# The own-row term of the node update as one 128-column matmul per pair, first of its group

## The chip, the cores and the metric

The kernel runs on one core of one Trainium2 chip. The metric is the device time of one execution in microseconds (us), lower is better. The engines are PE (matrix products; PEld is its loading of weights), DVE (vector), ACT (scalar), POOL (indirect DMAs here) and SP (DMA queue).

## The reference

A graph network of four layers over 6250 nodes of 64 features and 206250 edges sorted by destination. In each layer:

```
msg  = concat(h[src], h[dst]) @ WM + bM
mean, mx, mn, std, var, s = aggregates of msg over the edges of each destination node
agg  = concat(mean, mx, mn, std, var, s)
hu   = concat(h, agg, agg * amp, agg * att) @ WU + bU        # amp, att: one number per node
hbn  = batchnorm(hu / sqrt(n));  hm = leaky_relu(hbn @ Wmix + bmix)
h    = relu(batchnorm(hm + h)) + h
```

The first 64 rows of WU multiply the node's own row h; this product is what the change moves. The other 1152 rows multiply the aggregates, plain and scaled by amp and att.

## The kernel before, in words

The 6250 nodes are 50 tiles of 125. A tile j of the first half (j = 0 to 24) and its counterpart of the second half stand together as pair j: the transposed features hT hold the one in partitions 0 to 63 and the other in 64 to 127, and the weight blocks for the own row (W from column W_U0, 128 columns) and for the destination term (from W_BB) are block diagonal, so that 64 columns belong to each half a = 0, 1.

A layer has a dense stage (one-hot products on PE, running maxima on DVE, gathers by POOL) and then the node stage, the subject here: 25 pairs, unrolled in program order on each engine, followed by two batch norms. Layer 0 is written out by itself; layers 1 to 3 are one body in a hardware loop over l. There every semaphore wait compares with a register worked out from l, and the helper `wait` (L389 to L393) puts one more instruction, an increment of `passed`, behind each such wait. In layer 0 the values are constants and nothing is put behind.

For each pair PE runs, in this order (L1898 to L1906):
- `columns(j + 2)`: four transposes of the dense maxima and sums (L1854), then the destination product (L1858), which signals `t_ps`;
- `update(j, 0)`: waits for `hut_ev` (pair j - 2's result has been read out of the bank that is about to be written) and for `at_ev` (the transposed aggregates have been copied to SBUF), then three matmuls of 192 columns (L1882) and one of 64 columns (L1884);
- `features(j + 1)`: six transposes of the next pair's aggregates (L1870);
- `update(j, 1)`: the same four matmuls for the other half; the last one signals `u_ps`;
- `back(j - 1)`: waits for `hu_done`, then one transpose (L1893), which signals `ht_ps`.

A fp32 matmul appears as two passes in the trace (L1884: 4 layers x 25 pairs x 2 halves = 200 matmuls, 400 rows); a transpose as one.

DVE runs `gather_up(j + 3, j)` (L1548 to L1593): L1573 to L1592 gather the aggregates of pair j + 3 once `t_ps` is there, and between them L1538, L1543 and L1546 combine the update of pair j (`u_ps`) into hu and signal `hu_done`. ACT runs per pair the squares and roots (`moments`, L739 to L743), the copy of the transposed aggregates to SBUF (L751, `at_ev`), the read-out of the transposed result (L761, with its accumulator read; `hut_ev`) and a square of it (L770). In ACT's order L751 of pair j stands ahead of L761 of pair j - 2.

UPS are two PSUM banks used in turn: columns 0 to 191 of a bank belong to half 0 and 192 to 383 to half 1; of each 192, the first 64 take the own row. HPS, the transposed result, lies in the same bank behind them.

Of the kernel before, what the change touches and what calls it, by code (L numbers as in the profile page):

```python
# [12 lines left out]
P = 128  # L13
N = 6250
E = 206250
D = 64
# [7 lines left out]
NP = 125  # L24
# [116 lines left out]
W_BB, W_U0, W_MIX, W_BM, W_U, W_COL = 0, 128, 256, 384, 448, 1024  # L141
# [26 lines left out]
def build(nc, x, src, dst, WM, bM, WU, bU, gamma_t, beta_t, Wmix, bmix, gamma_o, beta_o, out):  # L168
# [14 lines left out]
    with ExitStack() as ctx:  # L183
        def sb(name, shape, dt=F32):
            return ctx.enter_context(nc.sbuf_tensor(name, shape, dt))
# [10 lines left out]
        hT = sb("hT", [P, FC])  # L196
# [3 lines left out]
        W = sb("W", [P, W_ALL])  # L200
# [29 lines left out]
        TPS, UPS, BPS = [bank[0], bank[1]], [bank[4], bank[5]], bank[6]  # L230
# [42 lines left out]
        aggT = [[v[:, k * 3 * NP:(k + 1) * 3 * NP] for k in range(2)] for v in (flat_rows, spare)]  # L273
# [115 lines left out]
        def wait(eng, s, value):  # L389

            wait_at(eng, s, value)
            if not isinstance(value, int):
                eng.sem_inc(S["passed"])  # L393

        def wait_at(eng, s, value):

            eng.wait_ge(S[s] if isinstance(s, str) else s, value)
# [1276 lines left out]
        def _(pe):  # L1674
# [18 lines left out]
            for m in range(BATCHES):  # L1693
# [3 lines left out]
                for j in range(j0, j0 + n):  # L1697
                    ins = nc.tensor.matmul(bank[m % 2][:, (j - j0) * NP:(j - j0 + 1) * NP], codev[0:NP, j, :], identb[0:NP, 0:NP],
                                           start=True, stop=True)
# [3 lines left out]
            for k in range(TILES):  # L1703
                pe.wait_ge(S["e_ready"], k + 1)
                row0 = 64 * (k // VROWS) + k % VROWS
                for m, r in enumerate(STEPS):
                    ins = nc.tensor.matmul(bank[m][:, 0:r.stop - r.start], SELW[:, SEL - row0:SEL - row0 + P], EB[k % EBLK][:, r],
                                           start=k == 0, stop=k == TILES - 1)
# [6 lines left out]
            for k in range(SCAN_CHUNKS):  # L1715
                nc.tensor.matmul(bank[k][:, 0:SCAN], ones_bf[:, :], onehot[:, k * SCAN:(k + 1) * SCAN],
                                 start=True, stop=True).then_inc(S["ps1"], 1)
            for k in range(SCAN_CHUNKS):
                pe.wait_ge(S["ps1_used"], k + 1)
                nc.tensor.matmul(bank[k][:, 0:SCAN], below_bf[:, :], onehot[:, k * SCAN:(k + 1) * SCAN],  # L1720
                                 start=True, stop=True).then_inc(S["ps2"], 1)
# [9 lines left out]
            def layer(l, stored):  # L1731
# [142 lines left out]
                def update(j, a):  # L1874

                    i = l * HALF + j
                    if a == 0 and j >= 2:
                        wait(pe, "hut_ev", i - 1)
                    wait(pe, "at_ev", 2 * i + a + 1)
                    u = UPS[j % 2][0:NP, a * 192:(a + 1) * 192]  # L1880
                    for c in range(3):
                        nc.tensor.matmul(u, aggT[j % 2][a][:, c * NP:(c + 1) * NP], W[:, W_U + c * 192:W_U + (c + 1) * 192],  # L1882
                                         start=a == 0 and c == 0, stop=False, skip_group_check=True)
                    ins = nc.tensor.matmul(u[:, 0:D], hT[:, j * NP:(j + 1) * NP], W[:, W_U0 + a * D:W_U0 + (a + 1) * D],  # L1884
                                           start=False, stop=a == 1, skip_group_check=True)
                    if a:
                        ins.then_inc(S["u_ps"], 1)

# [9 lines left out]
                for j in range(HALF):  # L1898
                    if j + 2 < HALF:
                        columns(j + 2)  # L1900
                    update(j, 0)
                    if j + 1 < HALF:
                        features(j + 1)
                    update(j, 1)
                    if j >= 1:
                        back(j - 1)  # L1906
# [46 lines left out]
```

## Time and profile before

| | |
|---|---|
| median of 3 runs | 3956.39 us (3953.85 to 3956.59) |
| profiled execution, span from first to last instruction | 3968.1 us (the page gives no other time for it) |
| PE busy | 3314.0 us, 84% |
| DVE busy | 3137.6 us, 79% |
| POOL busy | 2223.3 us, 56% |
| ACT busy | 1168.6 us, 29% |
| mean granted PE clock | 0.958 of full |

Busy shares are means over stages that have different limits. The node stages lie at about 1234 to 1349, 2077 to 2201, 2939 to 3063 and 3796 to 3920 us. In rows of a timeline, "x6" means six instructions in a row merged, with the start of the first; their durations overlap, so that the pace is read from one start to the next. In brackets stands how long the engine was idle before and who released it.

### The profile page before, as it was taken

The numbers are of one execution on the slowest core, as the hardware profiler recorded it, in microseconds if no ns is written. First come the engines' busy times: TensorE is split into PE (matmuls) and PEld (weight loads), VectorE is DVE, ScalarE is ACT, GpSimd is POOL, SyncE is SP. The second block draws the span as 40 slices with busy tenths as digits, with TensorE's granted clock in tenths as the row PEclk, the third lists the DMA queues.
The fourth block names the chain that finished last, engine by engine and source line by source line (L and its number), as shares of the span: only waits on it lengthen the run. The fifth ranks groups of instructions, "written<-read, shape, count | busy, mean of one in ns | idle before, by whom it ended". The sixth has DMA issues, their size and how long they took to land.

```text
span 3968.1 us, 88783 instructions
## 1 busy us (share of the span) xinstructions
PE 3314.0 (84%) x29640; PEld 2061.9 (52%) x29640; DVE 3137.6 (79%) x6027; ACT 1168.6 (29%) x3428; POOL 2223.3 (56%) x2221
## 2 busy tenths in 40 slices
PE   0055699898887799999998699999988799999986
PEld 0022344444446657555558456555557466655575
DVE  6598588788776778888877678888876788888876
ACT  4302122222223612222225322222225332222243
POOL 6402577666654037777753147777750177777640
PEclk9997899999998899999999899999999899999997
DMA  7003799889896056556672256566670366566750
GB/s 209 16 0 81 217 257 258 239 247 254 248 258 210 14 163 178 175 173 191 201 232 77 79 157 178 170 175 191 198 240 16 118 174 180 170 189 189 219 163 34
DMA packets 300094, 668.65 MB, mean 169 GB/s; under 512 B 81751, under 2 KB 180237, under 8 KB 296995
## 3 DMA queue, kind: packets, MB, share of 16 engines
q1 hardware_dynamic: 188676, 419.32, 35.4%
q0 software_dynamic: 78400, 192.26, 18.5%
q10 hardware_dynamic: 32732, 54.15, 3.9%
q14 instruction: 216, 1.77, 0.1%
q8 instruction: 70, 1.15, 0.1%
HBM read 517.78 MB, written 151.72 MB: 169 GB/s over the span
## 4 chain that ended last, share of the span: by engine, by line
PE 21%; issue 20%; DMA 18%; DVE 12%; POOL 12%; ACT 2%; SPq 1%; DVEq 1%; ACTq 0%; POOLq 0%
POOL rows L881 11%; DMA rows<-table,lists 10%; PE bank L1815 8%; DMA RE<-vd 6%; PE bank L1789 4%; PE bank L1882 4%; DVE accL L1438 2%; DVE scr L1361 2%; PE bank L1798 2%; DVE scr L1372 1%; DVE accL L1434 1%; PE bank L1870 1%; DMA RE<-ohd 1%; DMA left<-accL 1%; SPq L476 1%
## 5 line engine op out<-in xcount | busy, mean ns | idle before, releaser
L881 POOL DMA_INDIRECT rows<-table,lists x1828 | 1833.0, 1003 | 836.6 <-issue 518.1
L1815 PE MATMUL bank<-RE,split 125*64 125x482 bf16 x15600 | 1846.5, 370 | 18.9 <-ACT scr L605 18.9
L1815 PEld LDWEIGHTS bank<-RE,split 125*64 125x64 bf16 x15600 | 948.9, 111 | 691.0 <-issue 34.2
L632 ACT ACTIVATE split<-rows,masks 128x128 f32<-128x128 f32 x1828 | 600.1, 391 | 1693.5 <-DMA rows<-table,lists 1311.9
L1789 PE MATMUL bank<-RE,split 126*64 126x482 bf16 x7800 | 924.2, 372 | 79.8 <-DVE scr L1372 60.4
L1361 DVE TENSOR_TENSOR scr<-scr,bank 128x964 f32<-128x964 f32 x624 | 692.1, 1109 | 78.8 <-PE bank L1789 74.0
L1372 DVE TENSOR_TENSOR scr<-scr,bank 128x964 f32<-128x964 f32 x624 | 692.0, 1109 | 45.0 <-PE bank L1798 40.0
L1789 PEld LDWEIGHTS bank<-RE,split 126*64 126x64 bf16 x7800 | 471.6, 111 | 430.5 <-DVE scr L1372 67.1
L1798 PE MATMUL bank<-RE,flip_w 126*64 126x482 bf16 x2600 | 391.4, 373 | 112.8 <-DVE scr L1361 69.0
L1433 DVE TENSOR_TENSOR accL<-accL,rows 128x192 f32<-128x192 f32 (+2 forms) x664 | 224.6, 338 | 292.8 <-DMA rows<-table,lists 289.9
L1438 DVE TENSOR_TENSOR accL<-accL,split 128x384 f32<-128x384 f32 (+2 forms) x664 | 343.1, 517 | 1.7
L1798 PEld LDWEIGHTS bank<-RE,flip_w 126*64 126x64 bf16 x2600 | 152.0, 111 | 249.3 <-DVE scr L1361 93.6
L924 POOL DMA_INDIRECT accL<-left,nid x200 | 195.5, 977 | 99.4 <-issue 59.7
L1434 DVE TENSOR_TENSOR accL<-accL,rows 128x192 f32<-128x192 f32 (+2 forms) x664 | 221.5, 334 | 0.0
L1397 DVE TENSOR_SCALAR RE<-RE,col 126x2410 bf16<-126x2410 bf16 x130 | 115.1, 886 | 111.9 <-DMA RE<-vd 110.1
L864 POOL MEMSET accL<- 128x3328 f32 x4 | 11.5, 2872 | 337.2 <-DVE split L1344 334.7
L843 POOL DMA_INDIRECT pos_d<-accL,nid x50 | 54.4, 1087 | 230.6 <-DVE nid L1248 215.7
L1882 PE MATMUL bank<-W,rows 128*125 128x192 f32 x624 | 125.4, 338 | 41.9 <-ACT scr L761 41.9
L1882 PE MATMUL bank<-W,RE 128*125 128x192 f32 x576 | 113.1, 332 | 19.1 <-ACT scr L761 16.9
L1882 PEld LDWEIGHTS bank<-W,rows 128*125 128x125 f32 x624 | 101.2, 192 | 50.0 <-issue 40.2
L1573 DVE TENSOR_TENSOR rows<-bank,accL 125x256 f32<-125x256 f32 x100 | 42.5, 425 | 78.8 <-PE bank L1858 71.1
L1882 PEld LDWEIGHTS bank<-W,RE 128*125 128x125 f32 x576 | 90.7, 187 | 26.9 <-issue 23.9
(282 smaller groups left out, 2752.9 us busy)
## 6 DMA issues: line engine op xcount, KB each, us to landing
RE<-ohd SPq DMA_DIRECT2D x395, 593.1 KB
RE<-vd SPq DMA_DIRECT2D x130, 593.1 KB
ohd<-RE SPq DMA_DIRECT2D x130, 593.1 KB
rows<-table,lists POOLq DMA_INDIRECT x1828
left<-accL POOLq DMA_DIRECT2D x20, 1280.0 KB
dense_d<-scr ACTq DMA_DIRECT2D x104, 241.0 KB
split<-dense_d ACTq DMA_DIRECT2D x16, 625.0 KB, 6.5
table<-accL SPq DMA_DIRECT2D x36, 250.0 KB
```

The source lines that it names most:

```text
L632: ins = nc.scalar.activation(masked_rows[:, g % GM_RING * GC + k, :], ring[:, b * GC + k, :], ACT.Copy, scale=masks[:, m:m + 1])
L881: nc.gpsimd.indirect_dma_start(ring[:, b * GC + k, :], None, table, bass.IndirectOffsetOnAxis(ap=lists[:, c:c + 1], axis=0)).then_inc(col_ ...
L924: nc.gpsimd.indirect_dma_start(Lv[:, a, j, :], None, left, bass.IndirectOffsetOnAxis(ap=rank_i[:, i:i + 1], axis=0)).then_inc(l_ld[j // 5] ...
L1361: nc.vector.tensor_tensor(top, top, got, ALU.max).then_inc(S["g_top"], 1)
L1372: nc.vector.tensor_tensor(low, low, got, ALU.min).then_inc(S["g_used"], 1)
L1433: nc.vector.tensor_tensor(acc[:, :, 2 * D:3 * D], acc[:, :, 2 * D:3 * D], got[:, :, 0:D], ALU.max)
L1434: nc.vector.tensor_tensor(acc[:, :, 3 * D:4 * D], acc[:, :, 3 * D:4 * D], got[:, :, 0:D], ALU.min).then_inc(S["tops"], 1)
L1438: nc.vector.tensor_tensor(acc[:, :, 0:2 * D], acc[:, :, 0:2 * D], masked_rows[:, g % GM_RING * GC:g % GM_RING * GC + w, :], ALU.add).then_ ...
L1789: ins = nc.tensor.matmul(pair_bank(i, k)[half(k), 0:CH], split[0:NP + 1, k, q, 0:D], columns_of(k, NP + 1), start=q == 0, stop=q == 2)
L1798: ins = nc.tensor.matmul(pair_bank(i, k)[half(k), 0:CH], flip_w[0:NP + 1, :], columns_of(k, NP + 1), start=False, stop=True, skip_group_ch ...
L1815: ins = nc.tensor.matmul(SB[h * D:(h + 1) * D, 0:CH], split[0:NP, k, q, h * D:(h + 1) * D], columns_of(k, NP), start=k == 0 and q == 0, st ...
L1882: nc.tensor.matmul(u, aggT[j % 2][a][:, c * NP:(c + 1) * NP], W[:, W_U + c * 192:W_U + (c + 1) * 192], start=a == 0 and c == 0, stop=False ...
```

## The change

The three aggregate matmuls of each half are kept. The two own-row matmuls of 64 columns, one at the end of each half's group, are replaced by one of 128 columns whose output goes to both halves' first 64 columns (two runs of 64 with 128 columns between them). It stands at the start of the pair's group, behind the `hut_ev` wait and ahead of the `at_ev` wait, and carries `start=True`; the last aggregate matmul of half 1 now carries `stop` and the signal.

```diff
                     if a == 0 and j >= 2:
                         wait(pe, "hut_ev", i - 1)
+                    if a == 0:
+                        both = UPS[j % 2][0:NP, 0:384].rearrange("p (a s) -> p a s", a=2)[:, :, 0:D]
+                        nc.tensor.matmul(both, hT[:, j * NP:(j + 1) * NP], W[:, W_U0:W_U0 + P], start=True, stop=False, skip_group_check=True)
                     wait(pe, "at_ev", 2 * i + a + 1)
                     u = UPS[j % 2][0:NP, a * 192:(a + 1) * 192]
                     for c in range(3):
-                        nc.tensor.matmul(u, aggT[j % 2][a][:, c * NP:(c + 1) * NP], W[:, W_U + c * 192:W_U + (c + 1) * 192],
-                                         start=a == 0 and c == 0, stop=False, skip_group_check=True)
-                    ins = nc.tensor.matmul(u[:, 0:D], hT[:, j * NP:(j + 1) * NP], W[:, W_U0 + a * D:W_U0 + (a + 1) * D],
-                                           start=False, stop=a == 1, skip_group_check=True)
+                        ins = nc.tensor.matmul(u, aggT[j % 2][a][:, c * NP:(c + 1) * NP], W[:, W_U + c * 192:W_U + (c + 1) * 192],
+                                               start=False, stop=a == 1 and c == 2, skip_group_check=True)
                     if a:
                         ins.then_inc(S["u_ps"], 1)
```

## Rows read from the trace of the kernel before

**Rows 1.** Groups of instructions by line, whole run: busy us, mean ns | idle before.

```profile
L1884 PE MATMUL bank<-W,hT 128*125 128x64 f32 x400 | 66.1, 247 | 0.0
...
L1573 DVE TENSOR_TENSOR rows<-bank,accL 125x256 f32<-125x256 f32 x100 | 42.5, 425 | 78.8 <-PE bank L1858 71.1 <-DMA accL<-left,nid 5.3 <-DVE aggb L1592 1.7
```

**Rows 2.** Chain that ended last, layer 0's node stage: start us, us, what.

```profile
1292.65 1.24 PE bank L1882 x6
...
1296.71 0.43 DVE rows L1573
...
1299.26 0.32 ACT aggb L741
...
1300.82 0.37 ACT scr L761 x2
1301.23 1.24 PE bank L1882 x6
```

**Rows 3.** Timeline, layer 0: start us, us, engine line op, operands, count [idle before <-releaser].

```profile
1292.38 0.21 ACT L761 ACTIVATION_READ_ACCUMULATOR scr<-bank,W 128x1 f32 x1
...
1293.72 0.33 PE L1884 MATMUL bank<-W,hT 128*125 128x64 f32 x2
...
1293.89 0.81 PE L1870 MATMUL bank<-ident,aggb 125*128 125x125 f32 x6
...
1294.54 1.14 PE L1882 MATMUL bank<-W,rows 128*125 128x192 f32 x6
...
1295.51 0.33 PE L1884 MATMUL bank<-W,hT 128*125 128x64 f32 x2
...
1295.68 0.28 PE L1893 MATMUL bank<-ident,rows 125*128 125x125 f32 x1
...
1295.79 0.60 PE L1854 MATMUL bank<-ident,split 128*125 128x128 f32 x4
...
1296.23 0.38 PE L1858 MATMUL bank<-W,hT 128*125 128x128 f32 x2
```

**Rows 4.** Timeline, layer 1's node stage, two pairs.

```profile
2153.62 0.21 ACT L761 ACTIVATION_READ_ACCUMULATOR scr<-bank,W 128x1 f32 x1
...
2154.19 0.94 PEld L1882 LDWEIGHTS bank<-W,RE 128*125 128x125 f32 x6 [0.61 <-issue]
...
2154.22 1.21 PE L1882 MATMUL bank<-W,RE 128*125 128x192 f32 x6 [0.45 <-ACT scr L761]
...
2155.43 0.81 PE L1870 MATMUL bank<-ident,aggb 125*128 125x125 f32 x6
...
2158.62 0.42 DVE L1573 TENSOR_TENSOR rows<-bank,accL 125x256 f32<-125x256 f32 x1 [0.71 <-PE bank L1858]
...
2159.05 0.94 PEld L1882 LDWEIGHTS bank<-W,rows 128*125 128x125 f32 x6 [1.07 <-issue]
...
2163.46 0.62 PEld L1882 LDWEIGHTS bank<-W,RE 128*125 128x125 f32 x4 [0.63 <-issue]
```

**Rows 5.** Timeline, layer 0's end: one wait on a constant.

```profile
1346.81 0.29 DVE L1546 TENSOR_TENSOR rows<-rows,bank 125x128 f32<-125x128 f32 x1
...
1347.15 0.14 PEld L1893 LDWEIGHTS bank<-ident,rows 125*128 125x128 f32 x1 [1.31 <-DVE rows L1546]
```

**Rows 6.** Timeline, layer 1's start: one wait on a register, and two gathers.

```profile
2098.68 0.42 DVE L1573 TENSOR_TENSOR rows<-bank,accL 125x256 f32<-125x256 f32 x1 [1.61 <-PE bank L1858]
...
2101.02 0.28 DVE L1546 TENSOR_TENSOR rows<-rows,bank 125x128 f32<-125x128 f32 x1
...
2101.41 0.14 PEld L1893 LDWEIGHTS bank<-ident,rows 125*128 125x128 f32 x1
...
2102.94 0.42 DVE L1573 TENSOR_TENSOR rows<-bank,accL 125x256 f32<-125x256 f32 x1 [0.56 <-PE bank L1858]
```

**Rows 7.** Busy us of each engine, PEclk the granted clock, in 20 us of layer 1.

```profile
core 0: us, PE busy (x) PEld busy (x) DVE busy (x) ACT busy (x) POOL busy (x), PEclk, DMA share, GB/s
...
2140.00:2160.00 20.00, 16.68 (x122) 16.06 (x123) 16.26 (x61) 11.06 (x40) 0.00 (x0) 1.00 0.01 2
```

## The prediction

> **What bounds the kernel now.** I looked first at where the changed lines stand in the profile. The groups by line show that the own-row matmul costs PE no idle time of its own (L1884, idle before it 0.0), while DVE waited 71.1 us in all for the destination product L1858 ahead of its gather L1573 [rows 1]. So in the node stage DVE follows PE, and a shorter PE stretch can matter although DVE and PE are both busy most of the time.
>
> The chain of waits says how [rows 2]. It goes PE L1882 at 1292.65, DVE L1573 at 1296.71, ACT L741 at 1299.26, L761 at 1300.82, and PE L1882 again at 1301.23. The first L1882 is pair j, the last is pair j + 2: the loop covers two pairs in 8.58 us. Its PE segment (update of j, features of j + 1, the second update, back, columns of j + 3) takes 4.06 us, and its second segment (gather, moments, copy, read-out) 4.52 us. The other parity of pairs runs the same loop half a turn later. Neither engine is full: both wait in every turn, so what is taken from the PE segment comes off the loop, once in two pairs.
>
> In layer 1 the same loop is longer [rows 4]: L1882 starts to load at 2154.19, the gather starts at 2158.62, L1882 of pair j + 2 at 2163.46, in all 9.27 us. I use one such pattern for layers 1 to 3, which share the loop body. A layer of 25 pairs has 11 such turns, and behind the last gather the chain still goes through the updates of the last two pairs, which I count as one turn: 12 turns a layer, 48 in all.
>
> **What the passes cost.** In layer 0 from start to start [rows 3]: L1884 at 1293.72, next line at 1293.89, 0.17 us for two passes of 64 columns; the second half gives the same (1295.51 to 1295.68). Six passes of 192 columns take 0.97 (1294.54 to 1295.51) when nothing interrupts, 1.07 behind a wait (1292.65 [rows 2] to 1293.72), so a restart costs 0.10. Four passes of 128 columns take 0.44 (L1854 at 1295.79 to L1858 at 1296.23), 0.11 each. L1858 has the operands of the new matmul (hT as weights, 128 columns of W) and is two passes as well, so I price the new matmul at 2 x 0.11 = 0.22.
>
> **The change part by part, layer 0.**
> - Removed from update(j, 0): 0.17. Added ahead of it: 0.22. The restart is there before and after. First half: 1.24 us before (1292.65 to 1293.89), 0.10 + 0.22 + 0.97 = 1.29 after, 0.05 lost. The new matmul is not hidden in the wait: it stands behind `hut_ev`, and that is the wait that ends last (L761 releases it, and L751, which gives `at_ev`, is earlier in ACT's order).
> - Removed from update(j, 1): 0.17, nothing added. It shortens the way to back, columns and the next gather.
> - Together 0.12 a turn. 12 turns: 1.4 us.
>
> The output of the new matmul is in two runs of 64 columns. No row shows such a write from a matmul. Bounds: no price (0.22 for the pair of passes), or each run as dear as a separate pass of 64 (0.34, and the 0.12 is gone). I take no price, since the transposes and products of 125 to 192 columns all keep a pace by columns.
>
> The `stop` and signal now hang on a pass of 192 columns. A pass of it lasts longer than one of 64, but the signal `u_ps` releases only L1538, which stands behind the gather's L1573 except in the last pairs. There it is under 0.1 us a layer; I leave it out.
>
> **Layers 1 to 3.** Here the order of wait and matmul matters more. The accumulator read of L761 ends at 2153.83 (2153.62 + 0.21), and L1882 begins to load at 2154.19, 0.36 later [rows 4]; in layer 0 the same gap is 1292.59 to 1292.65, 0.06 [rows 2, 3]. The difference of 0.30 is what PE's sequencer spends on the two register waits and their increments. A single wait of this kind costs little: L1546 ends at 2101.30 and L1893 loads at 2101.41, 0.11 later [rows 6], against 0.05 where it is a constant (1347.10 to 1347.15) [rows 5]. So of the 0.36 some 0.12 belong to the first wait and 0.24 to the second with its register work.
> - After the change only the first wait stands ahead of PE's first matmul: the own row starts at 0.12 instead of 0.36.
> - The second wait is passed while the own row runs. It needs 0.24; the own row with the restart covers 0.10 + 0.22 = 0.32. I allow 0.06 for the issue of the own row's instructions ahead of the wait.
> - Before, L1870 starts 1.60 after the read's end (2155.43 - 2153.83). After: 0.12 + 1.29 + 0.06 = 1.47. Gain 0.13.
> - Update(j, 1): 0.17 as in layer 0. Together 0.30 a turn; 36 turns: 10.8 us.
> - Bounds of this term: if the second wait isn't hidden at all, the turn gains 0.12 as in layer 0 (with the own row unhidden), so 4.3 us; if its cover is complete, 0.36, so 13.0 us. I take 0.30, near the upper end, because the rows of the same body show waits being passed behind running matmuls: features stands behind three register waits and L1870 still follows without a gap (1.21 after L1882's first start of 2154.22, against 1.24 in layer 0) [rows 3, 4].
>
> **Does something else take it?** The gathers of two neighbouring pairs can't be nearer than DVE and `hu_done` allow. One place shows the limit: L1546 at 2101.02 releases back at 2101.41, and the gathers are then 4.26 apart (2098.68 to 2102.94) [rows 6]. Two pairs need 8.52 by that, and the turn would be 9.27 - 0.30 = 8.97. There is room. On DVE itself a gather with the combination keeps it busy for 16.26 of 20 us, PE 16.68, and PE had the full granted clock of 1.00 there [rows 7]. The end of a node stage sets the start of the next dense stage, so I carry the gain on one to one.
>
> **Sum.** 1.4 + 10.8 = 12.2 us. Against the profiled span of 3968.1 that is 3955.9. That execution was 0.3% longer than the median of the runs, which would scale a sum of 12 us by nothing, so I take it off the median: 3956.4 - 12.2 = 3944.2.
>
> A rule of the skill gives another price. The removed pair of 64-column passes kept a pace of 0.17, 0.085 a pass [rows 3]. The Trainium skill, "TensorE: Matmul & The Clock Gate", section "LDWEIGHTS (loading the stationary operand)", says that a weight load takes as many nanoseconds as it has columns, divided by 1.2, whatever the rows; for 125 columns that is 104 ns, and four removed loads against two added would be worth 0.21 a turn instead of 0.12, by an estimate from that page. The trace disagrees where the 64-column passes stand, so I stay with the rows.
>
> **Rivals.**
> 1. Small passes cost a full slot: the pace of 0.11, not 0.085, is what each removed pass gives back where loads follow one another without room. Then a turn gains 4 x 0.11 - 0.22 = 0.22 in layer 0 and 0.40 later: 2.6 + 14.4 = 17 us, 3939. For it speaks that L1870 and L1893, of 125 columns, show 0.11 too; against it the row of 0.17 [rows 3]. This is also the case to which the page's rule would lead.
> 2. Only the passes count: the sequencer's second wait is as long behind the own row as it was ahead. 48 turns x 0.12 = 5.8 us, 3950.6. For it: register work of 0.24 on one side against 0.22 of array time on the other is close.
> 3. Nothing comes out: the two-run output costs as two passes, or `hu_done` holds back() and the loop of the two parities absorbs the rest. 3956. Against it: the room of 9.27 to 8.52.
> 4. Slower: PE's sequencer passes the second wait, or its increment, only when the own row has left the array. A pass lasts 0.27 from its start, not 0.11 (L1884: 0.33 for two with the second 0.06 behind) [rows 3]. First half in layers 1 to 3: 0.12 for the first wait, 0.10 + 0.11 + 0.27 for the own row, 0.24 for the second wait, 0.10 restart and 0.97, in all 1.91, then L1870, against 1.60; less the 0.17 of the second half, 0.14 a turn lost, 5.0 us in 36 turns. Layer 0: 0.48 for the own row, 0.06 for a constant wait, 0.10 and 0.97, in all 1.61 against 1.24, less 0.17: 0.20 a turn, 2.4 us in 12. Together 7.4 us, 3963.8. It decides where the first half loses more than the 0.17 that the second gives back. Against it: L1870 follows L1884 without such a gap, with three waits between them.
>
> **How the numbers follow.** A change of under 0.2% (7.9 us) can't be told from none here. Chances: forecast 0.56, rival 1 0.06, rival 2 0.20, rival 3 0.10, rival 4 0.08. Faster by over 0.2% (below 3948.5) takes the forecast, rival 1 and a fifth of rival 2: 0.66. Slower by over 0.2% gets 0.08 from rival 4, whose 7.4 us lie at that bound, and from what no row shows. The same: 0.26. The range goes from rival 1 to just short of no change, 3939 to 3955, and leaves out rival 4, a part of rival 3 and little else.
>
> **What would show it.** In the timeline of layer 1, the own row must load about 0.12 behind the accumulator read of L761 and L1882 about 0.3 behind the own row; a gap of 0.5 or more is rival 4. In layer 0, from the own row to L1870 should be 1.29, and from the second L1882 to L1893 0.97 instead of 1.14. The turns should be 8.46 in layer 0 and about 8.97 later; if they stay at 9.27 while the PE stretch is shorter, rival 3 is right, and L1893 will be seen waiting for L1546. A granted clock below 1.00 in the middle of a node stage would make all of it wrong.

## The result, and the profile after

| | before | after |
|---|---|---|
| median of 20 runs | 3956.95 us | 3950.25 us |
| range | 3947.96 to 3972.60 | 3938.94 to 3964.58 |
| ratio after / before, 95% interval | | 0.9979 (0.9969 to 0.9989) |
| profiled span | 3968.1 us | 3940.5 us |

One of the 20 runs of the changed kernel took 4595.81 us at a granted clock of 0.75; it is in the median and neither in the range nor in the ratio.

The change made the kernel faster by 0.21%, 8.3 us of 3957 (4.4 to 12.3). I had forecast 12.2, at the very end of that interval. By its time alone the changed kernel (3950.25) lies nearer to rival 2 (3950.6) than to the forecast (3944.2). What tells the two apart is not the time but the turn, below. Two later comparisons of the same two kernels gave 0.9953 (0.9937 to 0.9969) and 0.9976 (0.9963 to 0.9989).

Two lengths carry what follows. A *turn* is two pairs of the node stage: the start of L1573 of the 25th gather less that of the 7th, divided by 9. The *node stages* are the sum over the four layers of the time from the first L1573 to the last L761. Both are worked out from the starts in the timelines.

| | turn, layer 0 | turn, layers 1, 2, 3 | node stages |
|---|---|---|---|
| before | 8.55 | 9.27, 9.28, 9.28 | 481.3 us |
| after | 8.43 | 8.94, 8.94, 8.93 | 466.9 us |

So the node stages lost 14.3 us: 2.3 in layer 0 and 4.4, 3.7 and 4.0 in the others. The two spans differ by 27.6. Most of the other 13.3 lies ahead of the first node stage, in code that the change doesn't touch: the first gather starts at 1221.1 in this profile, against 1234.2 before. In the other two profiles of the changed kernel (e1 and e9 below) it starts at 1223.9 and 1226.0, so this start scatters by some us. In between, from the end of one node stage to the start of the next, the three stretches add up to 2203.5 us before and 2203.7 after. Here are the totals of the changed kernel's profile (in them PE has 200 instructions fewer than before, x29640, two passes a pair), the group of L1573 with its waits, and that line's first and last start.

```profile
span 3940.5 us, 88360 instructions
...
PE 3300.3 (84%) x29440; PEld 2052.7 (52%) x29440; DVE 3138.4 (80%) x6027; ACT 1168.5 (30%) x3428; POOL 2228.9 (57%) x2221
```

```profile
L1573 DVE TENSOR_TENSOR rows<-bank,accL 125x256 f32<-125x256 f32 x100 | 42.5, 425 | 66.3 <-PE bank L1858 59.2 <-DMA accL<-left,nid 4.5 <-DVE aggb L1592 1.3
```

```profile
L1573 DVE TENSOR_TENSOR rows<-bank,accL x100: 424/425/427, 1221.1 to 3878.7; 125x256 f32<-125x256 f32 x100
```

The wait for L1858 fell from 71.1 us to 59.2 [rows 1], 11.9 us over the run, and DVE's work is what it was. In the changed file L1881 is the new matmul, L1885 the aggregate matmuls (L1882 before) and L1894 the transpose of back (L1893 before). The chain of waits, layer 0 (start us, us, what; compare [rows 2]), has the new matmul right behind L761:

```profile
1286.24 0.36 ACT scr L761 x2
...
1286.65 0.48 PE bank L1881 x2
1287.13 0.97 PE bank L1885 x6
1288.11 0.64 PE bank L1870 x6
1288.75 0.98 PE bank L1885 x6
1289.73 0.11 PE bank L1894
```

The timeline there (start us, us, engine, line, operands; compare [rows 3]):

```profile
1286.39 0.21 ACT L761 ACTIVATION_READ_ACCUMULATOR scr<-bank,W 128x1 f32 x1
...
1286.65 0.48 PE L1881 MATMUL bank<-W,hT 128*125 128x128 f32 x2 [0.72 <-ACT scr L761]
...
1286.97 1.14 PE L1885 MATMUL bank<-W,rows 128*125 128x192 f32 x6
...
1287.94 0.81 PE L1870 MATMUL bank<-ident,aggb 125*128 125x125 f32 x6
...
1288.59 1.14 PE L1885 MATMUL bank<-W,rows 128*125 128x192 f32 x6
...
1289.57 0.27 PE L1894 MATMUL bank<-ident,rows 125*128 125x125 f32 x1
```

L1881 to L1885 is 0.32, L1885 to L1870 0.97, in all 1.29 to L1870 against 1.24 before. The second half is 0.98 from L1885 to the transpose of back against 1.14. Layer 1, to be held against [rows 4]:

```profile
2135.53 0.42 DVE L1573 TENSOR_TENSOR rows<-bank,accL 125x256 f32<-125x256 f32 x1 [0.47 <-PE bank L1858]
...
2139.80 0.21 ACT L761 ACTIVATION_READ_ACCUMULATOR scr<-bank,W 128x1 f32 x1
2140.12 0.29 PEld L1881 LDWEIGHTS bank<-W,hT 128*125 128x125 f32 x2 [0.64 <-issue]
...
2140.15 0.45 PE L1881 MATMUL bank<-W,hT 128*125 128x128 f32 x2 [0.48 <-ACT scr L761]
...
2140.44 1.17 PE L1885 MATMUL bank<-W,rows 128*125 128x192 f32 x6
...
2141.44 0.81 PE L1870 MATMUL bank<-ident,aggb 125*128 125x125 f32 x6
...
2142.09 1.14 PE L1885 MATMUL bank<-W,rows 128*125 128x192 f32 x6
...
2143.06 0.27 PE L1894 MATMUL bank<-ident,rows 125*128 125x125 f32 x1
...
2144.44 0.42 DVE L1573 TENSOR_TENSOR rows<-bank,accL 125x256 f32<-125x256 f32 x1 [0.62 <-PE bank L1858]
```

L761's read ends at 2140.01 and L1881 loads 0.11 later, where L1882 loaded 0.36 behind it before. The second wait no longer shows: L1885 starts 0.32 behind the first load of L1881, which is what two passes of 128 columns with the restart take in layer 0. L1870 starts 1.43 behind the read's end, against 1.60. The second half is 0.97 from L1885 to L1894; in layer 1 before it was 1.14:

```profile
2156.08 1.14 PE L1882 MATMUL bank<-W,RE 128*125 128x192 f32 x6
...
2157.22 0.28 PE L1893 MATMUL bank<-ident,rows 125*128 125x125 f32 x1
```

The two L1573 rows are two gathers apart: a turn of 8.91 at this place.

The trace also has the sequencer's own instructions, and they show the second wait directly. L393 is the increment of `passed` that stands behind each register wait. Here are PE's two of them around these places (the line L393 of PE alone; a q behind an engine's name means its sequencer), before between 2153.8 and 2154.2 us and after between 2139.9 and 2140.4:

```profile
L393 PEldq EVENT_SEMAPHORE  x2: 51/51/51, 2153.9 to 2154.1; - x2
```

```profile
L393 PEldq EVENT_SEMAPHORE  x2: 51/51/51, 2140.0 to 2140.3; - x2
```

Before, both stand ahead of L1882's first load at 2154.19. After, only the first stands ahead of L1881's load at 2140.12, and the second comes at 2140.3, while the own row runs (2140.15 to 2140.60).

### The profile page after: what moved, and what is told of

It is laid out like the page before. It is cut to its first block, busy times and chain, and to the rows that moved or that the text cites. A ratio compares the mean times of both kernels' runs of the same rounds, so it can differ in the third digit from the quotient of the medians.

```text
span 3940.5 us, 88360 instructions
## 1 busy us (share of the span) xinstructions
PE 3300.3 (84%) x29440; PEld 2052.7 (52%) x29440; DVE 3138.4 (80%) x6027; ACT 1168.5 (30%) x3428; POOL 2228.9 (57%) x2221
## 4 chain that ended last, share of the span: by engine, by line
PE 22%; issue 19%; DMA 18%; POOL 12%; DVE 11%; ACT 3%; SPq 1%; DVEq 1%; ACTq 0%; POOLq 0%
POOL rows L881 11%; DMA rows<-table,lists 11%; PE bank L1815 8%; DMA RE<-vd 4%; PE bank L1789 4%; PE bank L1885 4%; DVE accL L1438 2%; DVE scr L1361 2%; PE bank L1798 2%; PE bank L1870 1%; DVE scr L1372 1%; SPq L476 1%; DVE accL L1434 1%; DMA left<-accL 1%; POOL accL L924 1%
## 5 line engine op out<-in xcount | busy, mean ns | idle before, releaser
L1885 PE MATMUL bank<-W,rows 128*125 128x192 f32 x624 | 122.2, 334 | 0.0
L1885 PE MATMUL bank<-W,RE 128*125 128x192 f32 x576 | 110.7, 328 | 0.7 <-ACT RE L751 0.7
L1885 PEld LDWEIGHTS bank<-W,rows 128*125 128x125 f32 x624 | 101.5, 192 | 0.0
L1573 DVE TENSOR_TENSOR rows<-bank,accL 125x256 f32<-125x256 f32 x100 | 42.5, 425 | 66.3 <-PE bank L1858 59.2
L1881 PE MATMUL bank<-W,hT 128*125 128x128 f32 x200 | 46.6, 315 | 54.3 <-ACT scr L761 54.1
```

Of the source, the lines that this page charges most:

```text
L1885: ins = nc.tensor.matmul(u, aggT[j % 2][a][:, c * NP:(c + 1) * NP], W[:, W_U + c * 192:W_U + (c + 1) * 192], start=False, stop=a == 1 and ...
```

## The experiments

The theory: in layer 0 the turn loses what the passes are worth; in layers 1 to 3 it loses in addition what the own row hides, which is the sequencer's work for the second wait. The rivals are that only the merge counts, or only the place, or that small passes have another price. The edits of e2 and e5 are shown against the kernel before, those of e3, e4, e6 and e7 against the changed kernel, and that of e8 against e7.

| run | turn, layer 0 | turn, layers 1 to 3 | node stages | less than before | ratio (95%) |
|---|---|---|---|---|---|
| e1, the change again | 8.43 | 8.94 | 465.7 | 15.6 | 0.9953 (0.9937 to 0.9969) |
| e2, merged, last | 8.43 | 9.16 | 475.0 | 6.2 | 0.9976 (0.9962 to 0.9989) |
| e3, two, first | 8.65 | 9.12 | 476.2 | 5.0 | 0.9981 (0.9966 to 0.9997) |
| e4, merged, behind both waits | 8.43 | 9.17 | 473.9 | 7.4 | 0.9986 (0.9967 to 1.0004) |
| e5, before, waits exchanged | 8.61 | 9.02 | 472.1 | 9.2 | 0.9978 (0.9963 to 0.9993) |
| e6, after, waits exchanged | 8.49 | 8.91 | 466.1 | 15.2 | 0.9955 (0.9940 to 0.9971) |
| e7, transposed result apart | 7.62 | 8.62 | 441.0 | 40.3 | 0.9896 (0.9875 to 0.9917) |
| e8, and back later | 7.60 | 8.14 | 425.1 | 56.2 | 0.9860 (0.9835 to 0.9885) |
| e9, the change a third time | 8.43 | 8.94 | 467.7 | 13.6 | 0.9976 (0.9963 to 0.9989) |

The time of a run scatters by 0.3% either way, mostly outside the node stages: the rest of the span was anything from 3465.6 to 3487.4 us in these eleven profiles, in no order with the edits. A turn comes back within 0.02 us in the three profiles of the changed kernel. So the turns decide between theories, and the ratios are only a rough check of the sum.

**e1 and e9, the change again.**

> The changed kernel once more, to see how far the 14.3 us that its four node stages became shorter in one profile (466.9 us in sum, 481.3 before, from the first L1573 to the last L761) return in the timed runs. Theory (the loop of two pairs shortens by 0.11 us in layer 0 and 0.34 in layers 1 to 3, and the rest of the kernel is untouched): node stages 466 to 468 us, turns 8.42 and 8.91, time 0.30 to 0.36% below before. Rival (part of the gain is given back in the dense stages behind): the same node stages, but the time only 0.1 to 0.2% below.

> The changed kernel a third time, since the first comparison gave 0.21% and the second 0.47%. Theory (the time falls by what the four node stages lose, 14 to 16 us of 3957): 0.36 to 0.40% below before, node stages 465 to 467 us, and the first two comparisons are scatter around it. Rival (a part is given back outside the node stages): 0.2% again at the same node stages.

The node stages are as in the first profile in both. The ratios are 0.47% and 0.24%. The gain of the node stages would be 0.39% in e1 (15.6 us), 0.34% in e9 (13.6) and 0.36% in the first comparison (14.3). It lies inside the intervals of e1 and e9 and just outside the first one's (at most 0.31%). On average the three comparisons say 12.1 us and the three profiles 14.5. So I can't rule out that 2 or 3 us are given back outside the node stages; the profiles show no place for it, and their scatter of 20 us outside would hide it.

**e2, the merge alone, last of the group.**

```diff
-                    ins = nc.tensor.matmul(u[:, 0:D], hT[:, ...], W[:, W_U0 + a * D:W_U0 + (a + 1) * D], start=False, stop=a == 1, ...)
                     if a:
+                        both = UPS[j % 2][0:NP, 0:384].rearrange("p (a s) -> p a s", a=2)[:, :, 0:D]
+                        ins = nc.tensor.matmul(both, hT[:, ...], W[:, W_U0:W_U0 + P], start=False, stop=True, ...)
```

> The merge alone: one matmul of 128 columns, but last in the second half's group, behind all waits, as the signal's carrier. Theory (passes are worth 4 x 0.085 - 2 x 0.11 = 0.12 a turn, the place is worth the other 0.22 in the looped layers): turns 8.41 in layer 0 and 9.13 in layers 1 to 3, node stages 475 to 476 us in sum, time 0.15% below before. Rival 1 (the merge is worth all of it, wherever it stands): 8.91 in the looped layers, 467 us. Rival 2 (a small pass costs a full slot of 0.11): 8.31 and 9.03.

A turn lost 0.12 in layer 0 and 0.12 in the others (9.28 to 9.16). The merge is worth 0.12 everywhere, as the theory has it, and both rivals are out: not 8.91, not 8.31 and 9.03.

**e4, the merged matmul first, but behind both waits.**

```diff
                     if a == 0 and j >= 2:
                         wait(pe, "hut_ev", i - 1)
+                    wait(pe, "at_ev", 2 * i + a + 1)
                     if a == 0:
                         both = ...
                         nc.tensor.matmul(both, ...)
-                    wait(pe, "at_ev", 2 * i + a + 1)
```

> The merged matmul first in the group, but behind both waits. Theory: as the merge alone, 8.41 and 9.13, L1870 starting 1.65 us behind the end of L761's accumulator read in the looped layers (0.36 + 0.10 + 0.22 + 0.97) against 1.43 in the changed kernel; node stages 475 to 476 us in sum. Rival (being first matters in itself, not the wait that it covers): 8.91 and 467 us.

The same as e2, 8.43 and 9.17. Layer 1 of this kernel, timeline (L1882 is the own row here):

```profile
2142.13 0.21 ACT L761 ACTIVATION_READ_ACCUMULATOR scr<-bank,W 128x1 f32 x1
...
2142.70 0.29 PEld L1882 LDWEIGHTS bank<-W,hT 128*125 128x125 f32 x2 [0.60 <-issue]
...
2143.02 1.14 PE L1885 MATMUL bank<-W,RE 128*125 128x192 f32 x6
...
2143.99 0.81 PE L1870 MATMUL bank<-ident,aggb 125*128 125x125 f32 x6
```

The read ends at 2142.34, the own row loads 0.36 later, and L1870 starts 1.65 behind the read's end, the figure expected. Against the changed kernel the one difference is on which side of the own row the second wait stands, and it is worth 0.23 a turn (9.17 to 8.94) in the looped layers and nothing in layer 0.

**e3, the place alone: two of 64 columns, first.**

```diff
                     if a == 0:
-                        both = ...
-                        nc.tensor.matmul(both, hT[:, ...], W[:, W_U0:W_U0 + P], start=True, ...)
+                        for b in range(2):
+                            nc.tensor.matmul(UPS[j % 2][0:NP, b * 192:b * 192 + D], hT[:, ...], W[:, W_U0 + b * D:W_U0 + (b + 1) * D], start=b == 0, ...)
```

> The place alone: the two matmuls of 64 columns stay two, but both stand between the two waits ahead of the pair's aggregate matmuls. Theory: no gain in layer 0, where a wait costs nothing (turn 8.53); in layers 1 to 3 the own rows start 0.24 us earlier and cover the second wait, so the turn is 9.25 - 0.24 = 9.0; node stages 473 us in sum, time 0.2% below before. Rival (the place is worth nothing, only the merge counts): 9.25 and 481 us.

Here the expectation missed: layer 0 became 0.10 slower a turn (8.65), and the looped layers gained 0.16, not the 0.24 that the place was to give. The timeline of layer 0:

```profile
1292.04 0.21 ACT L761 ACTIVATION_READ_ACCUMULATOR scr<-bank,W 128x1 f32 x1
1292.30 0.51 PEld L1881 LDWEIGHTS bank<-W,hT 128*125 128x125 f32 x4 [0.23 <-ACT scr L761]
1292.30 0.65 PE L1881 MATMUL bank<-W,hT 128*125 128x64 f32 x4
...
1292.73 0.95 PEld L1886 LDWEIGHTS bank<-W,RE 128*125 128x125 f32 x6
...
1293.81 0.81 PE L1870 MATMUL bank<-ident,aggb 125*128 125x125 f32 x6
```

From L1881 to L1870 it is 1.51. Less the restart of 0.10 and the 0.97 of the six passes, the four narrow passes took 0.44, 0.11 each, and not 0.085. The row of the loads shows the pace: L1886 begins to load 0.43 behind the first load of four. A narrow pass in a run of narrow passes costs what a pass of 128 columns costs. The turn of layer 0 says the same: this kernel has two passes more than the changed one, and its turn is 0.22 longer (8.65 against 8.43). So these four passes take 0.10 more in the new place than they gave back in the old one, which is the miss in layer 0, and about that of the looped layers. In the old place, at the end of the second half, the trace of before shows the two apart (a view of the stretch from 1295.75 on, which leaves the first one out):

```profile
1295.57 0.27 PE L1884 MATMUL bank<-W,hT 128*125 128x64 f32 x1
1295.68 0.28 PE L1893 MATMUL bank<-ident,rows 125*128 125x125 f32 x1
```

The first of the two starts at 1295.51 [rows 3]. So the narrow pass right behind a wide one took 0.06 to the next start and the second 0.11, as in a run. The 0.085 was the mean of two different passes.

**e5, before, with the waits exchanged.**

```diff
-                    if a == 0 and j >= 2:
-                        wait(pe, "hut_ev", i - 1)
                     wait(pe, "at_ev", 2 * i + a + 1)
+                    if a == 0 and j >= 2:
+                        wait(pe, "hut_ev", i - 1)
```

> The kernel before with nothing merged and nothing moved but the two waits of update exchanged: at_ev first, hut_ev second. Theory (in the looped layers 0.24 us of a turn is the sequencer's work for a second wait behind the one that ends last; the changed kernel covered it with the own row): the same 0.24 is to be had by passing at_ev while PE waits for hut_ev anyway, so turns 8.55 in layer 0 (unchanged) and 9.03 in layers 1 to 3, L1882 loading 0.11 to 0.12 behind the accumulator read's end instead of 0.36; node stages 472 to 473 us in sum. Rival (it is the place of the own row that counts, not the wait): 9.27 and 481 us.

The looped turn is 9.02, as expected: 0.26 from two lines exchanged, more than the merge gives. Layer 1, then layer 0:

```profile
2140.35 0.21 ACT L761 ACTIVATION_READ_ACCUMULATOR scr<-bank,W 128x1 f32 x1
2140.67 0.94 PEld L1882 LDWEIGHTS bank<-W,RE 128*125 128x125 f32 x6 [0.51 <-issue]
```

```profile
1290.70 0.21 ACT L761 ACTIVATION_READ_ACCUMULATOR scr<-bank,W 128x1 f32 x1
...
1291.03 0.94 PEld L1882 LDWEIGHTS bank<-W,rows 128*125 128x125 f32 x6 [0.80 <-ACT rows L751]
```

In layer 1 L1882 loads 0.11 behind the read's end (2140.56), against 0.36. In layer 0 it loads 0.12 behind it (1290.91), against 0.06, and the turn is 0.06 longer (8.61). That was not expected: of two waits on constants the order matters too. The sequencer's instructions show where the 0.06 goes. In this kernel PE has one instruction of its own for a wait (L397, where the waits are issued) between the read's end and L1882's load (a view of that line from 1290.90 to 1291.02):

```profile
L397 PEldq EVENT_SEMAPHORE  x1: 51/51/51, 1291.0 to 1291.0; - x1
```

It takes 0.05 us. In 21 pairs of layer 0, here and in e6, it stands ahead of the load every time; in the same 21 pairs of the kernel before and of the changed one it never does, and the load follows the read's end by 0.05 or 0.06. Why the release passes through an instruction of its own in this order is open. It isn't because no wait follows it: in the changed kernel, layer 0, no wait stands between `hut_ev` and the own row either, and its load comes 0.05 behind the read's end (1286.60 to 1286.65).

**e6, after, with the waits exchanged.**

```diff
+                    wait(pe, "at_ev", 2 * i + a + 1)
                     if a == 0 and j >= 2:
                         wait(pe, "hut_ev", i - 1)
                     if a == 0:
                         both = ...
-                    wait(pe, "at_ev", 2 * i + a + 1)
```

> The changed kernel with the two waits exchanged, so that both stand ahead of the own row, at_ev first. Theory (the second wait is wholly covered by the own row in the changed kernel): nothing changes, 8.43 and 8.94, node stages 466 to 467 us. Rival (a part of the wait still shows behind the own row): 0.05 to 0.1 less a turn in layers 1 to 3.

Layers 1 to 3 gained 0.03 (8.94 to 8.91), layer 0 lost 0.05 for the same reason as in e5. From the own row to L1870 it is 1.27 in layer 1, against 1.29 with the wait between them:

```profile
2137.88 0.45 PE L1882 MATMUL bank<-W,hT 128*125 128x128 f32 x2 [0.61 <-ACT scr L761]
...
2139.15 0.81 PE L1870 MATMUL bank<-ident,aggb 125*128 125x125 f32 x6
```

So the own row covers all but 0.02 of the wait of 0.25.

**e7, the transposed result in a bank of its own.** What makes update wait for L761 is only that the transposed result lies in update's bank.

```diff
-        HPS = [UPS[k][:, 6 * D:6 * D + NP] for k in range(2)]
-        FPS = [bank[k][:, 0:3 * NP] for k in (2, 3, 7)]
+        HPS = [bank[7][:, 0:NP] for k in range(2)]
+        FPS = [bank[k][:, 0:3 * NP] for k in (2, 3)]
...
-                    if a == 0 and j >= 2:
-                        wait(pe, "hut_ev", i - 1)          # in update
+                    if j >= 1:
+                        wait(pe, "hut_ev", i)              # in back, ahead of hu_done
```

The rings of FPS (`% 3`, and the `at_ev` count in features) become `% 2` and one tile nearer.

> The changed kernel with the transposed result in a bank of its own (bank 7; the transposed aggregates then use two banks instead of three), so that update needs no hut_ev wait and the own row is free to run while PE waits for at_ev. Theory (the read-out L761 leaves the loop, and the own row is hidden): layer 0 falls until PE's own pace binds, two pairs at 3.84 each, 7.7 a turn; layers 1 to 3 fall until the spacing of gathers by hu_done binds, two times 4.26, 8.5 a turn; node stages 443 us in sum, time 0.9% below before. Rival (with two banks for the transposed aggregates features waits for L751): 0.2 to 0.4 us a turn stay, 450 to 460 us.

7.62, 8.62 and 441.0 us: the theory, within about 0.1 a turn. In layer 0 the own row (L1879) runs right behind L1858 and no longer behind a wait:

```profile
1291.45 0.38 PE L1879 MATMUL bank<-W,hT 128*125 128x128 f32 x2
1291.68 0.42 DVE L1573 TENSOR_TENSOR rows<-bank,accL 125x256 f32<-125x256 f32 x1
...
1291.69 0.75 PE L1883 MATMUL bank<-W,RE 128*125 128x192 f32 x3
```

In layer 1 the next bound shows, as in [rows 6]: L1546 ends at 2121.53, back is released 0.11 later, after the loads of PE have stood for 0.60, and the gather follows 1.52 behind it.

```profile
2121.25 0.28 DVE L1546 TENSOR_TENSOR rows<-rows,bank 125x128 f32<-125x128 f32 x1
...
2121.64 0.14 PEld L1894 LDWEIGHTS bank<-ident,rows 125*128 125x128 f32 x1 [0.60 <-issue]
...
2123.16 0.43 DVE L1573 TENSOR_TENSOR rows<-bank,accL 125x256 f32<-125x256 f32 x1 [0.56 <-PE bank L1858]
```

**e8, and back behind the columns.**

```diff
                     if j + 2 < HALF:
                         columns(j + 2)
+                    if j >= 2:
+                        back(j - 2)
                     update(j, 0)
...
                     update(j, 1)
-                    if j >= 1:
-                        back(j - 1)
+                back(HALF - 2)
                 back(HALF - 1)
```

> As the one before, and back(j - 1) moved behind columns(j + 3), so that the next gather no longer stands behind the wait for hu_done. Theory (the spacing of 4.26 in layers 1 to 3 is that wait): the spacing falls to what PE's pace or DVE with its waits allow, 4.0 to 4.15, turns 8.0 to 8.3 in layers 1 to 3, 7.7 in layer 0; node stages 430 to 436 us. Rival (the spacing is DVE's own): no change against the one before.

8.14, in the range, and the rival is out. The node stages are 425.1 us, 5 below the range I gave. Median 3902.5 us, the fastest version tried, 1.40% below before. What binds now is DVE: it is idle for 0.34 ahead of L1573, and the releaser named is its own last instruction, so this is the time for its register waits; most gathers of this layer are 4.02 or 4.03 apart, as here. L1546 ends at 2122.47 and the transpose of back (L1894) follows at 2122.78 behind the columns, with no gather waiting for it any more. PE still waits ahead of L1883, but DVE no longer waits for PE here.

```profile
2119.86 0.42 DVE L1573 TENSOR_TENSOR rows<-bank,accL 125x256 f32<-125x256 f32 x1 [0.34 <-DVE aggb L1592]
...
2122.19 0.28 DVE L1546 TENSOR_TENSOR rows<-rows,bank 125x128 f32<-125x128 f32 x1
...
2122.78 0.14 PEld L1894 LDWEIGHTS bank<-ident,rows 125*128 125x128 f32 x1
...
2123.71 0.94 PEld L1883 LDWEIGHTS bank<-W,rows 128*125 128x125 f32 x6 [0.52 <-issue]
...
2123.88 0.42 DVE L1573 TENSOR_TENSOR rows<-bank,accL 125x256 f32<-125x256 f32 x1 [0.34 <-DVE aggb L1592]
```

## Why the prediction came out as it did

1. *The loop of two pairs sets the node stage; what PE's stretch loses comes off once a turn.* Right. The chain is the same after, with the same neighbours, and turns and stretches agree: in layer 1, 1.60 to 1.43 in the first half and 1.14 to 0.97 in the second are 0.34, and the turn lost 0.34.
2. *Layer 0: 0.12 a turn, 1.4 us.* The turn is right (8.55 to 8.43; 1.29 expected and found). The layer lost 2.3 us, more than the turns give. The third spacing of gathers was 4.24 before and 3.57 after, so about 0.7 of it lies at the head. That is scatter and no gain: in the three profiles of the changed kernel this spacing was 3.57, 3.14 and 4.03.
3. *The new matmul costs 0.22, its output in two runs of 64 columns nothing.* Right: 0.32 with the restart.
4. *Layers 1 to 3: 0.30 a turn, of which 0.12 are passes.* Right in kind, 0.34 in size. The first wait took 0.11 (0.12 expected). The allowance of 0.06 for the issue of the own row's instructions was not needed; e6 puts what is left of the wait at 0.02. e2, e4 and the change split the gain: 0.11 or 0.12 for the merge, 0.22 or 0.23 for the wait that it covers. The chain of 36 turns gave 12.1 us against 10.8.
5. *The price of the removed passes: 0.17 a pair, and not the estimate from the Trainium skill.* Right for where they stood, as the sum of the two; that each costs 0.085 is not. The estimate from the Trainium skill, "TensorE: Matmul & The Clock Gate", section "LDWEIGHTS (loading the stationary operand)", was 0.104 a pass. e3 shows 0.11 for narrow passes in a run, near that estimate. Two narrow passes as the tail of a group of wide ones cost 0.06 and 0.11 (and e2 gained 0.12 a turn, where 0.11 for each of the four would have given 0.22). So rival 1 is out for this change and right in e3.
6. *Nothing else takes it.* The room down to 4.26 between gathers was there: 4.34 and 4.57 in turn in the middle of layer 1 after. One of the two spacings of a turn does stand at 4.26 in many pairs (e1, layer 1: 4.26 and 4.66), but the other then takes the rest, and the turn is the same. Both stand near 4.26 only in e7, where it binds as described. From the 7th to the 25th gather of each layer the granted clock was 1.00 before and after.
7. *The sum: 12.2 us, 3944.2.* The node stages say 14.3, 15.6 and 13.6 in three profiles. The timed runs say 8.3, 18.6 and 9.5 with intervals of 4 to 6 us either way. The forecast lies within the third, at the upper end of the first (4.4 to 12.3) and just below the second (12.3 to 24.9). The second comparison excludes rival 2's 5.8 us, the first and the third allow it. Rivals 2 and 3 are out by the turns (0.12 or nothing in the looped layers), rival 4 by the gap of 0.29 between the own row and L1885, where it needed 0.5, and by the increment of the second wait, which comes while the own row runs. Rival 1 is out by the turns too: it asked for 0.22 in layer 0 and 0.40 later, against 0.12 and 0.34.

## What to carry to other kernels

When an engine stands before several waits, put the one that ends last at the end, and if that can't be, put a piece of work that needs only the first ones between: with register waits the one that ended last cost 0.11 us and each further one behind it 0.25, on the critical loop. With waits on constants the first of these two pieces of advice didn't pay: in layer 0 it cost 0.06 a turn (e5). Before shortening work on a loop, ask what makes the loop close: here it was a bank shared by two tensors, and parting them took another 26 us off the node stages, where the merge and the move together had taken 14 (e7 against the change). A price per instruction holds for its neighbours: measure it where it will stand.

## What I had not expected of the hardware

- Passes of 64 columns cost 0.06 and 0.11 us as the last two of a group of 192-column ones, 0.11 each as a run of four.
- Of two waits on constants, of which the first had long been met, the first load started 0.12 behind the read's end; with the met one behind the other, or behind the first matmul, it was 0.06 or 0.05 (e5 and e6 against the kernel before and the changed one). The difference is one sequencer instruction of 0.05 us ahead of the load; why it stands there is open.
